# Expert stage of a fused attention and mixture-of-experts layer: hand-overs between engines three steps apart, and a memset on the Pool behind every second scatter of results

## The reference

```python
x = x + attention(layernorm(x))
h = layernorm(x).reshape(4096, 256)
topv, topi = jax.lax.top_k(h @ gate_w.T, 8)          # 64 experts
rw = softmax(topv)
gate, up = split(einsum('nh,eih->nei', h, gu_w))     # 64 columns each
inter = silu(gate) * up * W[:, :, None]              # W: rw at topi, else 0
out = einsum('nei,ehi->nh', inter, dp_w)
x = x + out + sigmoid(h @ sh_gate1.T) * shared_expert(h)
```

## Time and profile before

| | before |
|---|---|
| median of three runs | 1210.2 us |
| lowest and highest run | 1207.94 and 1212.99 us |
| span of the profiled execution, first to last instruction | 1382.2 us |
| granted TensorE clock over the span | 0.909 of full speed |
| busy: PE, DVE, ACT, POOL | 78%, 51%, 47%, 52% |
| attention stage, last scatters, steps, tail (in the span) | 745, 64, 550, 23 us |

### The profile page before, as it was taken

One profiled execution on the slowest core, in us unless ns is written; L12 is line 12 of the kernel. 1 busy time (PEld: TensorE's weight loads), 2 busy tenths in 40 slices (PEclk: granted clock), 3 DMA queues, 4 the chain that ended last, 5 costly groups with the idle time before them and its releaser, 6 DMA issues.

```text
span 1382.2 us, 23533 instructions
## 1 busy us (share of the span) xinstructions
PE 1080.5 (78%) x7305; PEld 833.1 (60%) x7305; DVE 703.8 (51%) x2197; ACT 647.6 (47%) x1586; POOL 722.5 (52%) x953
## 2 busy tenths in 40 slices
PE   3799998888888888889765058887888878787875
PEld 1566666565565656566534047777777767676763
DVE  3476766666666666656525411121245544444447
ACT  2465656555555555655331024444445444444441
POOL 3111225657466564564566735655565565655552
PEclk9699999999999989989877569999999999998996
DMA  2586877212122121122228855555767777776536
GB/s 82 174 288 221 275 256 237 101 48 95 51 84 93 53 90 51 59 102 61 84 93 289 269 172 161 172 169 154 238 233 251 268 268 248 259 243 238 170 138 212
DMA packets 142824, 233.18 MB, mean 169 GB/s; under 512 B 17303, under 2 KB 119910, under 8 KB 137840
## 3 DMA queue, kind: packets, MB, share of 16 engines
q1 hardware_dynamic: 67936, 101.06, 22.7%
q0 software_dynamic: 27600, 69.28, 14.1%
q10 hardware_dynamic: 47168, 61.35, 13.5%
HBM read 107.32 MB, written 132.53 MB: 174 GB/s over the span
## 4 chain that ended last, share of the span: by engine, by line
PE 46%; DVE 16%; another core or an unknown queue 14%; issue 13%; ACT 8%; POOL 1%; DMA 1%; ACTq 0%; SPq 0%; DVEq 0%; POOLq 0%
PE psB L1412 6%; DVE nmax L868 6%; PE psD L1429 5%; PE psv L607 4%; PE ps L511 4%; PE psA L1402 4%; PE ps L558 3%; PE ps L518 3%; PE psp L490 3%; PE psp L504 3%; PE psC L1420 3%; ACT xT L1297 2%; ACT y L1313 2%; PE psq L634 2%
## 5 line engine op out<-in xcount | busy, mean ns | idle before, releaser
L1497 POOL DMA_INDIRECT res_d<-y,dst_i x319 | 320.9, 1006 | 231.9 <-ACT y L1313 117.8
L463 POOL DMA_INDIRECT rows_d<-pay,slot_i x256 | 256.5, 1002 | 75.4 <-issue 73.4
L868 DVE TENSOR_REDUCE nmax<-ps 128x1 f32<-128x512 f32 (+3 forms) x448 | 225.8, 531 | 135.8 <-PE ps L518 93.5
L736 ACT ACTIVATE wgu_s<-ps 128x512 f32<-128x512 f32 x320 | 191.9, 600 | 123.4 <-PE ps L518 91.3
L1216 DVE TENSOR_TENSOR inner<-inner,psB 128x128 f32<-128x128 f32 x160 | 45.8, 286 | 316.8 <-ACT inner L1302 250.5
L1429 PE MATMUL psD<-wdp_s,innerT 128*128 x638 | 174.8, 397 | 21.1 <-ACT innerT L1306 17.6
L1412 PE MATMUL psB<-wgu_s,xT 128*128 x1276 | 179.1, 285 | 1.2 <-ACT xT L1297 0.8
L518 PE MATMUL ps<-mask,ident_b 128*128 128x256 bf16 (+1 forms) x640 | 175.4, 274 | 0.4 <-issue 0.4
L511 PE MATMUL ps<-kT,qT 96*128 96x512 f32 (+3 forms) x512 | 168.3, 391 | 8.1 <-DVE nmax L868 4.8
L558 PE MATMUL ps<-qT,kT 128*128 128x512 f32 (+3 forms) x512 | 165.8, 387 | 4.9 <-ACT wgu_s L736 4.2
L1412 PEld LDWEIGHTS psB<-wgu_s,xT 128*128 128x128 f32 x1276 | 163.9, 201 | 1.8 <-issue 1.2
(11 more groups left out here) (256 smaller groups left out, 1620.0 us busy)
## 6 DMA issues: line engine op xcount, KB each, us to landing
rows_d<-blank ACTq DMA_DIRECT2D x8, 5440.0 KB, 19.3
xg<-rows_d SPq DMA_DIRECT2D x160, 272.0 KB
yk<-res_d SPq DMA_DIRECT2D x28, 1024.0 KB
wgu_s<-wgu_in ACTq DMA_DIRECT2D x8, 1024.0 KB
x_d<-x SPq DMA_DIRECT2D x30, 192.5 KB
xs<-x_d SPq DMA_DIRECT2D x30, 192.5 KB, 2.5
res_d<-y,dst_i POOLq DMA_INDIRECT x319
wgu_s<-x_in SPq DMA_DIRECT2D x32, 128.0 KB, 2.2
```

The costliest lines, as they stand in the source:

```text
L463: pool.indirect_dma_start(rows_d, bass.IndirectOffsetOnAxis(ap=slot_i[par][:, t, k:k + 1], axis=0), pay[par][:, t, :], None).then_inc(s_sc ...
L736: act.activation(pexp[p % 4][:, s, :], ps2[:, (5 * p + s) % 2, :], ACT.Exp, scale=HEAD_D ** -0.5).then_inc(s_exp, 1)
L868: return dve.tensor_reduce(nmax[u][:, tile, heads[0]:heads[-1] + 1], src, AX.X, ALU.max, negate=True)
L1497: pool.indirect_dma_start(res_d, bass.IndirectOffsetOnAxis(ap=dst_i[:, j % (2 * G):j % (2 * G) + 1], axis=0), y[:, j % Y, :], None, bounds ...
```

## The change

`GATE, TURN, DOWN` go from 2, 4, 6 to 3, 6, 9. The second pair's brought-forward steps, the loads and the sums of tiles move along with them. Three waits are added on the PE that the old distances implied: `turn_x` waits for `xT_copy` of two pairs earlier, `gate_up` for `gated` and `turn_inner` for `innerT_copy` of two pairs earlier. PSUM banks and SBUF buffers stay as they are. On the Pool a memset of a scratch tile of 128 x 256 follows every second indirect DMA, 159 in all; each waits for the memset before it.

```diff
@@ -988,7 +988,7 @@
             PAIRS = BLOCKS // 2
             G, R, Y, A = 16, 4, 10, 3
-            GATE, TURN, DOWN = 2, 4, 6
+            GATE, TURN, DOWN = 3, 6, 9
@@ -997,6 +997,7 @@
             dst_i = sb("dst_i", [P, 2 * G], I32)
+            pause = sb("pause", [P, D], F32)
@@ -1015,6 +1016,7 @@
             e_front, e_back = sem("pe_step_front"), sem("pe_step_back")
+            e_paused = sem("pool_paused")
@@ -1030,13 +1032,13 @@
             STEPS = PAIRS + DOWN + 4
-            SOONER = {GATE: (1, 2), TURN: (2, 4), DOWN: (3, 6)}
+            SOONER = {GATE: (1, 3), TURN: (2, 5), DOWN: (3, 7)}
...
-            LOADED_BEFORE, SUMMED_AFTER = 26, 12
+            LOADED_BEFORE, SUMMED_AFTER = 32, 15
@@ -1397,6 +1399,8 @@
                 def turn_x(i):
                     pe.wait_ge(e_x[i % (G // 2)], 16 * (2 * i // G + 1))
+                    if i >= 2:
+                        pe.wait_ge(e_a, i - 1)
@@ -1406,6 +1410,8 @@
                 def gate_up(i):
                     pe.wait_ge(e_a, i + 1)
+                    if i >= 2:
+                        pe.wait_ge(e_in, i - 1)
@@ -1416,6 +1422,8 @@
                 def turn_inner(i):
                     pe.wait_ge(e_in, i + 1)
+                    if i >= 2:
+                        pe.wait_ge(e_c, i - 1)
@@ -1497,6 +1505,10 @@
                     pool.indirect_dma_start(
                         res_d, bass.IndirectOffsetOnAxis(ap=dst_i[:, j % (2 * G):j % (2 * G) + 1], axis=0), y[:, j % Y, :], None,
                         bounds_check=ROUTED - 1, oob_is_err=False).then_inc(e_out[j % Y], 16)
+                    if j % 2 == 1:
+                        if j > 1:
+                            pool.wait_ge(e_paused, j // 2)
+                        pool.memset(pause[:], 0.0).then_inc(e_paused, 1)
```

## The result

The changed kernel took 1243.97 us (median of four runs, 1241.32 to 1245.11), the kernel before 1209.07 us beside it (four runs). The ratio is 1.0275, with a 95% interval of 1.0255 to 1.0294: 33 us slower, 31 to 36; the two medians are 34.9 us apart. The forecast was 1239 us.

What follows compares the result with a forecast made beforehand. The Pool's queue of result DMAs was taken to bound the timed steps, at or near. Steps of 426.0 + 5.4 (filling) + 31.4 (memsets) = 462.8 us, plus 809.0 - 56 and 23.2, gave 1239 us; range 1195 to 1258.

Steps and rivals of the forecast that it cites:

- the odd trace: Profiled execution of the kernel before: span 1382.2 us against a run median of 1210.2, so 172 us not in the runs.
- The hold-ups: Idle time put down to another core or unknown queue: 64 us in the first 745, 129 in the steps; mostly not in runs.
- A: What the timed run saves ahead of 809 us of the trace: 48 to 64 us, 56 taken.
- the rival in which the memset lets the PE's counts through: Pool operation behind every second DMA ends hold-ups early, if timed DMAs are 1.15 us apart or less: 1190 us, chance 0.17.
- The Pool's queue: Result DMAs in the expert steps, starts 1.29 us apart, at or near the bound of the timed steps, 426 to 442 us.
- The term of the memset: Between result DMAs on the Pool: 0.20 us more for each of 157 memsets behind the third pair, 31.4 us.
- The filling: Third pair's `down` moves from step 8 to 11 at 1.78 us a step, so the Pool's steady queue begins 5.4 us later.
- The distances: Longer distances in the steps buy only 0.22 us more cover with two banks; costed at nothing.
- The floor of 426: Pool's least time for the steps: third pair's first DMA 20.9 us after 809, then 314 starts 1.29 us apart, 405 us.
- The memset hides, or the Pool has slack: Rival: memset lies in the 0.30 us of issue between the Pool's DMAs; 1210 to 1217, say 1213 us; chance 0.20.
- Still slower: Rival: the DMA behind every memset takes 1.09 us, 17 us more, 1256 us; chance 0.05.
- The Trainium skill's rule on occupancy: Most-contended engine has the highest occupancy; the Pool at 52% has room, the memset is free, 1210 to 1217 us.

Runs made afterwards that it cites:

- experiment 1: Kernel before, unchanged, profiled again (the second profile of before): 1209.95 us, span 1208.2 us.
- experiment 2: Changed kernel without the memset on the Pool, distances 3, 6, 9 and the three waits kept: 1214.48 us, ratio 1.0037 to the kernel before.
- experiment 3: Kernel before with the memset behind every second result DMA alone, distances 2, 4, 6: 1236.41 us, ratio 1.0219.
- experiment 9: Kernel before with result DMAs that check no bounds, padded rows going to 2048 spare rows: 1202.37 us, ratio 0.9924.
- experiment 5: Kernel before with result DMAs of 64 rows in place of 128, half of the results not written: 1193.05 us, ratio 0.9850.
- experiment 6: Changed kernel without the memset, with result DMAs of 64 rows in place of 128: 1195.90 us, ratio 0.9892 to the kernel before.
- experiment 4: Changed kernel with a memset of 128 x 8 in place of 128 x 256: 1213.80 us, ratio 1.0027 to the kernel before.
- experiment 12: Kernel before with result DMAs that check no bounds, measured a second time: 1204.42 us, ratio 0.9944.

## Why the prediction was right, point by point

**The reading of the odd trace held.** The hold-ups show in none of the later traces, whose spans are those of the runs. The second profile of before is 174 us shorter than the first, beside the 193 us that the forecast read and the 172 by which the runs were shorter. A was taken as 56 us, the middle of a range; it is 52 to 56 by the first `turn_x`. (The 64 us ahead of the steps are not the Pool's alone, as the forecast read them: the DVE is busy 22 of them. Nothing in the sum hangs on that.) Where the hold-ups came from stays open: no run showed them again. With them gone, nothing was left for the rival in which the memset lets the PE's counts through, and its own condition, a spacing of 1.15 us or less, was not met either (1.29).

**The Pool's queue was the bound, as said.** A microsecond put into it or taken out of it came out in most of the time: 26 to 29 us more by the memsets, 33 more by larger ones, and 7 to 9 less by a queue 9 us shorter. In the traces of experiments 1, 2, 3, 9 and of after, the Pool is never idle for longer than 0.31 us from the third pair's first DMA to the last. The forecast's "at or near" is the right word: below some 414 us the PE takes over (experiment 5), so 18 us is what there was to gain here from the Pool alone.

**The term of the memset was a little large.** It was 0.20 us for each, 0.19 rounded up, from the spacing over a 0.74 us addition. Measured were 0.18 in steady operation (1.47 in place of 1.29), and over the queue 28.7 us (after beside experiment 2) or 26.2 (experiment 3 beside 1) in place of 31.4. Two errors partly cancel in the 0.18: this memset is busy 0.35 us, not 0.31, but starts 0.02 us before the DMA's end and not 0.02 behind it. 157 x 0.184 are 28.9 us, so the 28.7 are the steady price. The 26.2 are less because the queue of before was 7.4 us longer than 314 x 1.29, and that of experiment 3 only 4.5 us longer than 157 x 2.765: 43 of the DMAs are busy over 1.06 us in experiment 1 and 27 in experiment 3. Why the number differs was not tried.

**The filling was nearly right, by a sum with two parts.** 5.4 us were forecast for the third pair, 3 steps of 1.78 us. From the first `y_copy` to the third are now 14.3 us, in the timeline of ACT after, in place of 8.4 in experiment 3, 5.9 more:

```profile
763.26 0.59 ACT L1315 COPY y<-psD 128x512 f32<-128x512 f32 x1 [1.16 <-PE psD L1437]
770.50 0.58 ACT L1315 COPY y<-psD 128x512 f32<-128x512 f32 x1
777.56 0.58 ACT L1315 COPY y<-psD 128x512 f32<-128x512 f32 x1 [0.33 <-PE psC L1428]
```

But the first `down` now stands ahead of the second pair's `gate_up`, and so it and its `y_copy` come 1.7 us sooner (this `y_copy` 8.85 us behind the first `turn_x`, 10.53 in experiment 3), which the forecast left out. Net are 4.2 us, and 4.5 in the time of experiment 2.

**The distances are worth nothing in the steps, as said.** They change nothing in the queue (experiment 2), and they give nothing where the Pool is not in the way (experiment 6). Two banks and the 0.22 us of extra cover fit that; that a third bank would have helped was not tried, and with no late hand-over left to cover there is no reason to expect it.

**The sum came 5 us short, by errors that partly cancel.** The terms for the change were 31.4 + 5.4 = 36.8 us, more than the 33 to 35 measured. But they were added to a base of 809 - 56 + 426.0 + 23.2 = 1202 us, 8 below the median of before. Part by part, the forecast beside the trace of after:

| part | forecast, us | after, us |
|---|---|---|
| up to the first `turn_x` | 753.0 | 754.41 |
| from there to the third pair's first DMA | 26.3 | 24.57 |
| from there to the last result DMA | 436.5 | 440.35 |
| from there to the end | 23.2 | 21.67 |
| span | 1239.0 | 1241.0 |

The largest error is in the queue. The floor of 426 took every DMA at 1.29 us, and so the floor of a queue was used as its length. Without the memset the queue lasts 411.7 us (experiment 2), not 405.1: the mean spacing was 1.314 in experiment 1, almost all of it because 43 of its 315 DMAs are busy over 1.06 us, up to 1.25. Against that stand a memset term, a start of the queue and an end that were each 1.5 to 3 us too long. A run's time is another 1.8 us above its span, which a sum built on a span leaves out. That these come to no more than 5 us is in part luck. Taken from the median itself, the same terms would have given 1247. The range, 1195 to 1258, covered both.

**The rivals.** "The memset hides, or the Pool has slack" (1213 us) fell: it hides up to some 0.15 us (experiment 4), and this one is 0.35. "Still slower", with DMAs of 1.09 us behind every memset, is not in the timeline: they take 0.98. The Trainium skill's rule on occupancy (Perfetto Trace Analysis, Identifying the Most-Contended Engine) would have put the Pool, at 60% in the second profile of before, behind the PE, which that section judges among others by its weight loads, 67% busy there. The trace doesn't agree for the Pool: at 60% busy over the span, and 74% in the steps (320.7 of 430.5 us), its queue was worth 7 to 9 us for 0.03 us a DMA (experiments 9 and 12), since the 0.30 us between two DMAs can't be used beyond one short operation.

## What to carry to other kernels

Judge a queue of indirect DMAs by the distance of their starts and not by the engine's busy share, and put the length that was measured, not the number times the best spacing, into the sum. An operation put between two of them is free only as far as it fits in the gap that is there; the rest is paid once for each. When the profiled execution is longer than the runs, look for what repeats in it and is too long to be in them, take it out, and see whether the bound that is left gives the time of the runs.

## What the runs showed of the hardware

An indirect DMA's price on the Pool hardly depends on its rows: 128 rows are busy 0.98 us and 64 rows 0.91, with 0.30 us behind either. So a row costs about 0.001 us (0.07 / 64) and the instruction some 1.1 us with its gap. The Trainium skill (GPSIMD Engine Reference, Elementwise — side-by-side cycle accounting) counts a dispatch in software for each instruction of this engine. A memset of 8 columns that is busy 0.15 us, while one of 256 takes 0.35 and one of 512 takes 0.57, agrees with a fixed part of some 0.14 us; that this part is the dispatch no run here shows. Memsets of the same three sizes elsewhere in these traces, with no result DMA right ahead of them, are busy 0.10, 0.31 and 0.51 us, so behind a DMA each takes some 0.04 to 0.05 us more.

Without the bounds check a DMA is 0.02 us shorter and the next starts 0.03 us sooner, though more rows are written. And the gap in front of a DMA is 0.30 us behind another DMA, but 0.16 behind a memset of 128 x 256 and 0.18 behind one of 128 x 8: a memset in between takes the place of nearly half of the gap. What the gap consists of was not tried.
